# Full-height contraction in the second value-projection matmul of a cross-attention kernel

## The reference, cut to what matters

```
n, c, s = 16, 64, 256;  h = 8
xn  = (x - mean) * rsqrt(var + eps) * gamma + beta        # mean and var per sequence n
q   = Wq xn + bq;   k, v = Wkv context + bkv              # 8 heads of 64 channels
att = softmax(q^T k / sqrt(64), axis=keys)                # n, h, 256 x 256
y   = att v                                               # n, h, 256, 64
out = x + Wo y + bo
```

## Time and profile before

| | |
|---|---|
| three runs | 258.68, 258.95, 259.62 us (median 258.95) |
| span of the profiled execution, first to last instruction | 255.2 us |
| mean granted TensorE clock | 0.979 |
| busy: PE, PEld, DVE, ACT, POOL | 229.4, 203.3, 211.6, 203.2, 198.5 us |
| instructions of PE | 2746 matmuls, 2746 weight loads |
| L450 and L451 | 32 matmuls each, 15.7 and 16.2 us busy |

### The profile page before, as it was taken

How to read it: one execution, slowest core, us unless ns; L and a number is a source line. 1 busy time by engine, 2 the same in 40 slices (tenths; PEclk the granted TensorE clock), 3 DMA queues, 4 the chain that set the end, 5 groups by cost and what they waited for, 6 DMA issues and landing times.

```text
span 255.2 us, 8140 instructions
## 1 busy us (share of the span) xinstructions
PE 229.4 (90%) x2746; PEld 203.3 (80%) x2746; DVE 211.6 (83%) x446; ACT 203.2 (80%) x391; POOL 198.5 (78%) x188
## 2 busy tenths in 40 slices
PE   0571969999999999999999999999999999999982
PEld 0571747888898889888888898888888889888871
DVE  2399998899988888888888888888888888887875
ACT  2343345999899999999999999999999989998970
POOL 3047968577999797979797979797979888989580
PEclk9999996899999999999999999999999999999997
DMA  6999402010111111112121212121212121010000
GB/s 141 215 293 213 98 0 84 25 52 14 53 44 55 44 55 38 56 31 62 32 62 32 62 32 62 32 62 32 62 32 62 33 64 35 13 32 13 13 4 22
DMA packets 13412, 15.08 MB, mean 59 GB/s; under 512 B 2064, under 2 KB 11920, under 8 KB 13200
## 3 DMA queue, kind: packets, MB, share of 16 engines
q1 hardware_dynamic: 13072, 14.16, 20.9%
q10 hardware_dynamic: 320, 0.66, 1.2%
HBM read 5.90 MB, written 1.05 MB: 27 GB/s over the span
## 4 chain that ended last, share of the span: by engine, by line
PE 71%; DVE 17%; DMA 4%; issue 3%; ACT 2%; POOL 2%; SPq 0%; POOLq 0%
PE ps_sc L380 12%; PE ps_max L399 11%; PE ps_sc L381 10%; PE ps_t L362 7%; PE ps_z L416 6%; PE ps_z L418 5%; PE ps_m L451 5%; PE ps_z L417 5%; PE ps_t L363 5%; DMA x_res<-x_tiles 4%; DVE neg_max L733 4%; PE ps_m L450 4%; DVE t_b L717 3%; DVE x_all L644 2%; DVE x_seq L644 1%
## 5 line engine op out<-in xcount | busy, mean ns | idle before, releaser
L605 POOL TENSOR_TENSOR p_lo<-p_full,p_hi 128x512 f16<-128x512 f32 x122 | 144.9, 1194 | 32.6 <-ACT p_full L525 31.2
L733 DVE TENSOR_REDUCE neg_max<-ps_max 128x2 f32<-128x512 f32 x128 | 84.5, 664 | 0.0
L523 ACT ACTIVATE p_hi<-ps_sc 128x512 f16<-128x512 f32 x128 | 76.1, 595 | 5.0 <-PE ps_sc L381 0.6
L525 ACT ACTIVATE p_full<-ps_sc 128x512 f32<-128x512 f32 x128 | 76.6, 599 | 0.6 <-POOL p_lo L605 0.6
L380 PE MATMUL ps_sc<-t_a,c_seq 128*128 128x256 f32 x256 | 73.0, 306 | 0.0
L381 PE MATMUL ps_sc<-t_b,c_seq 65*128 65x256 f32 x256 | 67.6, 284 | 0.0
L416 PE MATMUL ps_z<-u_hi,p_hi 128*128 128x65 f16 x512 | 60.8, 196 | 1.2 <-POOL p_lo L605 1.0
L417 PE MATMUL ps_z<-u_lo,p_hi 128*128 128x64 f16 x512 | 59.6, 193 | 0.0
L418 PE MATMUL ps_z<-u_hi,p_lo 128*128 128x65 f16 x512 | 59.3, 193 | 0.0
L416 PEld LDWEIGHTS ps_z<-u_hi,p_hi 128*128 128x128 f16 x512 | 45.6, 97 | 7.3 <-DVE z_n L740 0.7
L380 PEld LDWEIGHTS ps_sc<-t_a,c_seq 128*128 128x128 f32 x256 | 49.3, 193 | 0.7 <-issue 0.6
(11 more groups left out here) (100 smaller groups left out, 310.6 us busy)
## 6 DMA issues: line engine op xcount, KB each, us to landing
ctx_raw<-ctx SPq DMA_DIRECT2D x8, 256.0 KB, 16.4
c_seq<-c_all SPq DMA_DIRECT2D x16, 128.0 KB, 2.0
x_seq<-x_all SPq DMA_DIRECT2D x14, 128.0 KB, 2.0
c_max<-c_all SPq DMA_DIRECT2D x14, 128.0 KB, 2.0
x_res<-x_tiles SPq DMA_DIRECT2D x4, 256.0 KB, 7.1
z_n<-ctx_flat SPq DMA_DIRECT2D x1, 1024.0 KB, 13.6
c_seq<-c_all SPq DMA_DIRECT2D x16, 64.0 KB, 2.0
out<-x_res SPq DMA_DIRECT2D x16, 64.0 KB, 1.7
```

Source lines behind the costliest of these rows:

```text
L523: nc.scalar.activation(p_hi[:, buf, :, :].rearrange("p t s -> p (t s)"), scores, ACT.Exp).then_inc(act_phi, 1)
L525: nc.scalar.activation(p_full[:, head % 2, :], scores, ACT.Exp).then_inc(act_p, 1)
L605: nc.gpsimd.tensor_tensor(p_lo[:, buf, :, :].rearrange("p t s -> p (t s)"), p_full[:, head % 2, :], p_hi[:, buf, :, :].rearrange("p t s -> ...
L733: nc.vector.tensor_reduce(neg_max[:, (par + dn) % 2, head, :], ps_max[:, head % 2, :].rearrange("p (t s) -> p t s", t=KT), X, ALU.max, neg ...
```

## The change

The second matmul of each u step contracts over 128 rows where it contracted over 64. Rows 64 to 127 of `b_w[:, 1]` are set to zero once by DVE at the program's start, so the rows of ones in `c_seq` slot 1 add nothing. PE waits for that memset once, ahead of the first u step. The order of instructions on PE, ACT, POOL and SP is as before, and DVE has one more at its start.

```
                         if kt == 0:
                             need(pe, dma_cseq[q], 32)
                             need(pe, pool_b, 3)
+                            need(pe, dve_ones, 3)
                             need(pe, act_mt, 1)
...
                     mm(ps_m[:], c_seq[:, q, 0, keys], b_w[:, 0, :], start=True, stop=False)
-                    mm(ps_m[:], c_seq[0:C, q, 1, keys], b_w[0:C, 1, :], start=False, stop=True).then_inc(pe_u, 1)
+                    mm(ps_m[:], c_seq[:, q, 1, keys], b_w[:, 1, :], start=False, stop=True).then_inc(pe_u, 1)
...
             nc.vector.memset(x_seq[C:P, :, 1, :].bitcast(fp32), 1.0).then_inc(dve_ones, 1)
             nc.vector.memset(c_seq[C:P, :, 1, :].bitcast(fp32), 1.0).then_inc(dve_ones, 1)
+            nc.vector.memset(b_w[C:P, 1, :].bitcast(fp32), 0.0).then_inc(dve_ones, 1)
```

## The result

| | before | changed |
|---|---|---|
| median of four runs | 258.81 us (256.62 to 259.62) | 245.56 us (245.39 to 246.81) |
| ratio | | 0.9501, 95% interval 0.9454 to 0.9548 |
| span of the profiled execution | 255.2 us | 243.9 us |
| time of the profiled execution | not given | 245.67 us |

The kernel became 5% faster. The span of the profile, for which the prediction gave "about 244.0", came out at 243.9. What stood between the span and the time was wrong; the span was hit, though not by every term of its sum.

The account below looks back on a forecast made before the run. PE's stream was taken to bound the kernel, with gaps at height changes. Savings of 10.0 + 0.75 + 0.4 = 11.15 us take the span from 255.2 to about 244.0 and the median from 258.95 to 247.7, range 245.9 to 250.0.

Parts of the forecast that it names:

- half the gap stays: Rival, chance 0.05: 512 columns delay a load for their own reason, one of two gaps per u step remains; 253.4 us.
- nothing changes: Rival, chance 0.03: `c_seq`, `b_w` or PSUM accumulation separates the u step's matmuls, height is irrelevant; time stays 258.9 us.
- slower: Rival, chance 0.02: full-height load cannot start before the matmul ahead ends, its whole 0.19 us is open; 268 us.
- the take-over: Rival, chance 0.05: small waits in ACT's order do not close, the sequence settles at 12.6 us; about 252 us.
- the third to fifth step: U steps ahead of 69.81 us: DVE's chain turns PE's saving into longer waiting; counted 0, 1.2 us without that cover.
- The memset is hidden: Added 64 x 512 memset, 0.48 us, lies under DVE's idle time before the first `x_tiles`; 0.5 us without that cover.
- first to sixth u step: First two u steps at the low clock: 0.55 and 0.20 us saved, sum 0.75, bounds 0.3 and 1.0.
- The steady term: 25 u steps from 69.81 to 226.69 us, each 0.40 us shorter: 10.0 us saved, 9.0 to 10.8.
- The term for the last two u steps: Half a step, 0.2 us, saved at each by L451 ending earlier for `u_hi`: 0.4 us, bounds 0 and 0.8.

## Why the prediction was right and wrong

**Right: the cause and its size per step.** The gaps were put down to the change between 64 and 128 rows, 0.40 us per u step with bounds 0.36 and 0.43. Measured: 0.387. The rivals "half the gap stays", "nothing changes" and "slower" are refuted by the timeline after; the runs with 256 columns, with two 64-row matmuls in a row and with 65 rows leave the change between 64 and more rows as the only cause.

**Right: PE stays the bound.** 12.28 us per sequence was forecast, 12.30 came, and between 75 and 225 us the list of waits has no row for PE. Behind that there is one thing that the forecast did not have. The chain of work that ended last lay on PE with 71% of the span before and 2% on POOL; now it is 52% and 13%, and from about 184 to 225.7 us it runs over POOL's `p_lo` (L606). There, between the last two u steps, stands PE's first wait for it, which the kernel before does not have at that place:

```profile
225.72 0.19 PE L416 MATMUL ps_z<-u_hi,p_hi 128*128 128x65 f16 x1 [0.30 <-POOL p_lo L606]
```

So POOL has almost no slack left at the end, and a further gain on PE would meet it. ACT's margin was enough; the take-over did not come. DVE's waits shrank instead: before `u_lo` they came to 14.3 us from 51 us to the end, after 19.2 before the change.

**Right: what counted as nothing.** DVE's chain still covers the third to fifth step. PE waited 1.7 us for `t_b` in 40 to 70 us, after waiting 0.5 us. The memset is hidden.

**Wrong: the step from the span to the time.** The prediction said: "the median of the runs, 3.75 us above that span, goes from 258.95 to about 247.8". This took 3.75 us as work outside the first and last instruction. It is 1.8 us. The other 2 us belonged to the start of other, longer executions than the profiled one: in the second profile of before the span is 1.6 us longer, and all of it lies ahead of the sixth u step (71.43 against 69.81). This step alone puts the forecast outside: with 1.8 us, the forecast span of 244.0 gives 245.8 us for an execution with that start; the four timed ones have a median of 245.56 and the profiled one 245.67.

**Wrong: the width.** "The three runs of before lie within 0.94 us, so I widen by 0.4". Sixty-two executions of before lie between 255.4 and 261.9 us, and sixteen of the changed kernel between 245.0 and 248.7. Three runs did not show this spread, and that the profile's span lay 3.75 us below them could have been the hint that there was one.

**Partly luck: the span.** It was forecast to 0.1 us, but the terms were not that good. Between the two profiles that the prediction compares, the 11.27 us lie as follows:

| stretch | predicted | measured |
|---|---|---|
| up to the start of the first u step | 0 | 0.30 |
| first to sixth u step | 0.75 | 1.52 |
| sixth to thirty-first (25 steps) | 10.0 | 9.67 |
| thirty-first to the end | 0.4 | -0.22 |

The steady term is the one that the argument was about, and it is right to 0.33 us. The term for the last two u steps was wrong: the last two starts lie 4.78 us apart in both kernels, and behind the last it is 17.59 us before and 17.81, 17.39 and 17.39 after, so between -0.2 and 0.2 was gained. The forecast took 0.2 us for each of these u steps; of the 0.39 us that the last but one saves, PE now waits 0.30 for `p_lo`. What was missing there came from a start that was 1.8 us shorter instead of 0.75, and the two starts differ in their clock too: it was low for 5.7 us behind the first u step before and for 2.3 after. In the profiles in which the low clock ends soon, the first five steps are worth 0.3 to 0.4 us; whether 0.75 is right for a start like the one that the prediction read is open.

**The gain over many executions.** The executions that the ratios compare have medians of 257.0 us (47 of before, those with a known span) and 246.1 (16), a difference of 11.0 beside the forecast 11.15; over all 62 of before it would be 12.3. Of this, 9.5 to 10.0 us lie behind the start of the sixth u step (185.34 less 175.38 to 175.89). So the prediction had the gain; what it had wrong was to take the span from one execution and the time from others.

## What to carry to other kernels

When a matmul with half the array's height stands alone in a dense stream of full-height ones, look at whether the weight loads next to it wait for "issue": here each change of height cost 0.193 us at the full clock, and zero rows, whose memset did not show in the time, removed it. Group matmuls of one height, or pad the odd one, but only where PE's stream is the bound.

Before a sum from one profile is turned into a time, compare the span with the time of that same execution. If it isn't known, a difference between the span and the other runs may be another start, and the range must be as wide as the starts are.

## What the runs showed of the hardware that was not expected

- The same kernel reached its sixth u step anywhere between 68.4 and 74.8 us, if the part behind it took 185.34 us in each of the 58 executions, as it did in both that were profiled.
- One small DVE instruction (`u_bound`, L709) took 2.21 to 2.25 us in six profiles and 0.15 to 1.02 in eight. In the six it stood beside a POOL instruction and ended with it.
- The page's row of granted clock shows 9 from the first slice on, but the weight loads of 128 columns before about 33 us record 0.33 us, as in the stretch granted 0.50, against 0.19 us later. The low clock reaches further back than that row says. In the profile with the memset alone the row is silent until 45 us, and so its mean granted clock of 0.993 tells nothing of the start.
- Time less span is 1.7 to 2.1 us in all 58 executions of before whose span is known, but 2.2 to 3.0 in 13 executions of kernels with 65 or 128 rows in the loop (ten on one chip, three on another). Why is open; no run was made for it.
